# Taking a pair's two rounds of products apart, with the spread of the row sums between and behind them

## What is computed

```
h1     = concat(k, g, outer(k, g))            # 32 + 32 + 1024
act    = sigmoid(h1 @ W1 + b1)                # 36 hidden units
weight = act @ W2 + b2                        # one number for each goods row
out    = sum over the 200 rows of g * weight  # [2048, 32]
```

## Time and profile before

| | us |
|---|---|
| median of 3 runs | 266.45 (266.11 to 266.81) |
| profiled execution, its own time | 265.84 |
| span of the profiled execution | 264.0 |
| PE busy | 252.4 |
| ACT busy | 236.6 |
| POOL busy | 196.8 |
| DVE busy | 193.7 |

### The profile page before, as it was taken

How to read it: one execution, slowest core, us unless ns; L and a number is a source line. 1 busy time by engine, 2 the same in 40 slices (tenths; PEclk the granted TensorE clock), 3 DMA queues, 4 the chain that set the end, 5 groups by cost and what they waited for, 6 DMA issues and landing times.

```text
span 264.0 us, 18277 instructions
## 1 busy us (share of the span) xinstructions
PE 252.4 (96%) x7492; PEld 148.1 (56%) x7492; DVE 193.7 (73%) x1108; ACT 236.6 (90%) x658; POOL 196.8 (75%) x349
## 2 busy tenths in 40 slices
PE   7998999999999999999999999999999999999960
PEld 2425656555656656666556566566665565665640
DVE  0890277677778777777777787787787777877886
ACT  2897999999999999999999999999999999999840
POOL 1300787778888888888888888888888888888872
PEclk9999999999999999999999999999999999999997
DMA  5881767767777788777677787787777787777200
GB/s 207 263 298 38 218 190 217 219 203 241 216 227 237 216 240 234 217 235 224 220 237 217 235 230 222 233 233 215 233 226 219 233 233 229 226 222 232 63 0 11
DMA packets 38196, 54.84 MB, mean 208 GB/s; under 512 B 4241, under 2 KB 37905, under 8 KB 38033
## 3 DMA queue, kind: packets, MB, share of 16 engines
q1 hardware_dynamic: 37872, 54.15, 68.1%
q10 hardware_dynamic: 288, 0.32, 0.4%
HBM read 54.19 MB, written 0.26 MB: 206 GB/s over the span
## 4 chain that ended last, share of the span: by engine, by line
PE 91%; ACT 2%; DMA 2%; DVE 2%; POOL 1%; issue 0%; POOLq 0%; DVEq 0%
PE z_ps L337 29%; PE w_ps L384 27%; PE x_ps L360 16%; PE s_ps L422 6%; PE x_ps L422 6%; PE z_ps L289 2%; ACT act L498 2%; DMA act<-w_outer 2%; PE s_ps L337 2%; DVE goods L538 2%; PE s_ps L289 1%; PE x_ps L289 1%; PE x_ps L302 1%; PE w_ps L289 0%; POOL top L255 0%
## 5 line engine op out<-in xcount | busy, mean ns | idle before, releaser
L498 ACT ACTIVATE act<-z_ps,bias 128x200 f32<-128x200 f32 x448 | 149.8, 440 | 10.7 <-PE z_ps L337 4.3
L538 DVE CUSTOM_DVE_ANT_0 goods<-s_ps,goods 128x200 f32<-128x200 f32 x248 | 80.5, 362 | 30.9 <-PE w_ps L422 30.9
L337 PE MATMUL z_ps<-goods,wm_ring 32*32 32x200 f32 x3360 | 78.1, 339 | 0.1
L255 POOL TENSOR_SCALAR top<-whole,consts 128x200 bf16<-128x200 f32 x64 | 50.1, 783 | 21.7 <-DVE whole L530 15.6
L337 PEld LDWEIGHTS z_ps<-goods,wm_ring 32*32 32x32 f32 x3360 | 44.7, 103 | 20.1 <-issue 11.3
L384 PE MATMUL w_ps<-act,consts 128*32 128x200 f32 x1008 | 55.7, 339 | 0.0
L538 DVE CUSTOM_DVE_ANT_0 goods<-x_ps,goods 128x200 f32<-128x200 f32 x124 | 40.4, 364 | 20.6 <-PE s_ps L422 20.6
L360 PE MATMUL x_ps<-goods,wx 128*32 128x200 f32 x1024 | 55.3, 333 | 0.0
L259 POOL TENSOR_SCALAR mid<-rest,consts 128x200 bf16<-128x200 f32 x64 | 50.1, 783 | 6.3
L538 DVE DVE_READ_ACCUMULATOR2_ANT out_stage<- 128x1 f32 x512 | 42.7, 83 | 0.0
L422 PE MATMUL s_ps<-stack,pick_sb 64*128 64x200 bf16 x248 | 42.3, 251 | 0.0
(11 more groups left out here) (53 smaller groups left out, 210.6 us busy)
## 6 DMA issues: line engine op xcount, KB each, us to landing
goods<-goods_t SPq DMA_DIRECT2D x256, 200.0 KB, 2.9
act<-cand_r SPq DMA_DIRECT2D x1, 1024.0 KB, 5.3
act<-cand_u SPq DMA_DIRECT2D x1, 256.0 KB, 2.7
out_t<-out_stage SPq DMA_DIRECT2D x4, 64.0 KB, 2.4
consts<-small ACTq DMA_DIRECT2D x1, 164.5 KB, 5.3
act<-w_outer ACTq DMA_DIRECT2D x1, 144.0 KB, 5.5
pick_sb<-pick SPq DMA_DIRECT2D x1, 128.0 KB, 2.6
```

The costliest lines, as they stand in the source:

```text
L255: nc.gpsimd.tensor_scalar(top[:, :], whole[:, q % 2, :], m1, None, ALU.mult).then_inc(part_step, 1)
L337: last = nc.tensor.matmul(z_bank(slot, r)[32 * c:32 * c + 32, N * s:N * s + N], weights(slot, 32 * r, 4 * s + c), goods[32 * r:32 * r + 32 ...
L498: last = nc.scalar.activation(act[:, p % A_SLOTS, r, N * s:N * s + N], z_bank(p, r)[:, N * s:N * s + N], ACT.Sigmoid, bias=bias[:, r, p, s ...
L538: last = nc.vector.tensor_tensor_reduce(goods[:, q % G_SLOTS, v, :], s_bank(q, f, s)[:, N * i:N * i + N], goods[:, q % G_SLOTS, v, :], 1.0 ...
```

## The change

- In `products` the rounds are separate calls. The order on PE is now: round 0, spread f = 0, round 1, spread f = 1, `row_sums`, `products_x`.
- The spread has other banks: `w_ps` and `s_ps[1]` for f = 0, `x_ps` and the fourth bank of the pair before for f = 1. So round 0 waits, beside `goods_loaded` and `z_read`, for `pooled[1][1]` of the pair before; `products_x` waits for `pooled[1][0]` and `row_sums` for `pooled[0][0]` of the same pair's spread.
- DVE takes both halves of `pool_units` first and `keep` after them.
- `wm` is laid out in twos of hidden units: one copy of a bank now writes every second element, and a copy to the ring reads and writes neighbours in twos. Pairs 0 to 3 read the ring too; DVE fills their four places (`of_ring`), and raises `ring_filled`.
- GpSimd's operations are as before.

The core of the diff:

```diff
-        wm = sb("wm", [P, UNITS // RUN, HM, RUN])
+        wm = sb("wm", [P, UNITS // RUN, HM // 2, RUN, 2])
...
+        def s_banks(q, f):
+            if q + LAG >= PAIRS:
+                z0, z1, z2, z3 = (z_ps[:, r, :] for r in range(4))
+                return (((z0, z1), (z2, z3)), ((s_ps[1], x_ps), (z0, z1)), ((z2, z3), (s_ps[1], x_ps)))[q + LAG - PAIRS][f]
+            return ((w_ps, s_ps[1]), (x_ps, z_bank(q + LAG - 1, 3)))[f]
...
-            def products(p, slot, loaded):
+            def products(p, slot, s, loaded=None):
                 pe.wait_ge(pick_loaded, 16)
-                pe.wait_ge(goods_loaded[slot % G_SLOTS], loaded)
-                if slot >= 1:
-                    pe.wait_ge(z_read, p)
-                for s in range(2):
-                    ...
+                if s == 0:
+                    pe.wait_ge(goods_loaded[slot % G_SLOTS], loaded)
+                    if slot < FILL:
+                        pe.wait_ge(ring_filled, slot + 1)
+                    if slot >= 1:
+                        pe.wait_ge(z_read, p)
+                    if slot >= LAG + 1:
+                        pe.wait_ge(pooled[1][1], p)
+                ...
...
-                    products_x(p, slot)
-                    spread(p, slot, 1)
+                    products_x(pe.snap(pair, min_val=FILL - 1, max_val=PAIRS - 1), slot)
...
-                    products(p, slot + 1, pe.snap(loaded, min_val=64, max_val=64 * (TURNS + 1)))
+                    products(p, slot + 1, 0, pe.snap(loaded, min_val=64, max_val=64 * (TURNS + 1)))
                     spread(p, slot + 1, 0)
+                    products(p, slot + 1, 1)
+                    spread(p, slot + 1, 1)
                     row_sums(p, slot + 1)
...
+            for p in range(FILL):
+                if p == 2:
+                    keep_biasx()
+                nc.vector.tensor_copy(*of_ring(p)).then_inc(ring_filled, 1)
...
                 if q >= 0:
                     pool_units(q, 0)
-                if 1 <= p <= PAIRS:
+                    pool_units(q, 1, PAIRS - 1 if p == PAIRS else None)
+                if 1 <= p < PAIRS:
                     keep(p - 1)
-                if q >= 0:
-                    pool_units(q, 1)
```

More of the change, by code:

```diff
@@ L134, in wm_units, with of_ring @@
         def wm_units(h):
-            return wm[:, :, h, :]
+            return wm[:, :, h // 2, :, h % 2]
         def wb_runs(i, x):
             return wb_bank(i, x).rearrange("j (a b) -> j a b", b=RUN)
+        def of_ring(p):
+            first = p * PAIR_U % RUN
+            units = wm[:, p * PAIR_U // RUN, :, first:first + PAIR_U, :]
+            return (wm_ring[:, p % RING, :, :].rearrange("j u (g e) -> j u g e", e=2),
+                    units.rearrange("j g u e -> j u g e"))
         consts_loaded = sem("consts_loaded")
@@ L153, in build @@
         bias_kept = sem("bias_kept")
+        ring_filled = sem("ring_filled")
         z_done = sem("z_done")
@@ L314, in _ @@
             pe.wait_ge(pick_loaded, 16)
[L318 to L323, removed]
-            def products(p, slot, loaded):
-                pe.wait_ge(pick_loaded, 16)
-                pe.wait_ge(goods_loaded[slot % G_SLOTS], loaded)
-                if slot >= 1:
-                    pe.wait_ge(z_read, p)
-                for s in range(2):
[L335 to L342, removed]
+            def products(p, slot, s, loaded=None):
+                pe.wait_ge(pick_loaded, 16)
+                if s == 0:
[6 more added lines that the diff above has]
+                        pe.wait_ge(pooled[1][1], p)
+                for r in range(4):
+                    for c in range(4):
+                        last = nc.tensor.matmul(z_bank(slot, r)[32 * c:32 * c + 32, N * s:N * s + N],
+                                                wm_ring[32 * r:32 * r + 32, slot % RING, 4 * s + c, :],
+                                                goods[32 * r:32 * r + 32, slot % G_SLOTS, 4 * s + c, :],
+                                                start=True, stop=True)
+                    if s == 1:
+                        last.then_inc(z_done, 1)
             def products_x(p, slot):
@@ L351, in products_x @@
                 if slot >= LAG:
-                    pe.wait_ge(pooled[0][0], p)
-                elif slot >= 1:
-                    pe.wait_ge(actx_done, p)
+                    pe.wait_ge(pooled[1][0], p)
                 for s in range(2):
@@ L383, in row_sums @@
                             left, right = w2x[:, t, :], actx[:, a, :]
-                        last = nc.tensor.matmul(sums_bank(slot - 1)[32 * t:32 * t + 32, 0:N], left, right,
+                        last = nc.tensor.matmul(w_ps[32 * t:32 * t + 32, 0:N], left, right,
                                                 start=step == 0, stop=step == 2)
@@ L421, in spread @@
                         rows = slice(64 * s, 64 * s + 64)
-                        last = nc.tensor.matmul(s_bank(q, f, s)[:, N * i:N * i + N], pick_sb[rows, 2 * f + i, :],
+                        last = nc.tensor.matmul(s_banks(q, f)[s][:, N * i:N * i + N], pick_sb[rows, 2 * f + i, :],
                                                 stack[rows, q % 2, :], start=True, stop=True)
@@ L426, in _ @@
             for p in range(FILL):
-                products(p, p, 64)
+                products(p, p, 0, 64)
                 if p >= LAG:
                     spread(p, p, 0)
+                products(p, p, 1)
+                if p >= LAG:
+                    spread(p, p, 1)
                 if p >= 1:
@@ L479, in to_ring @@
             def to_ring(p):
-                first = p * PAIR_U % RUN
-                if p >= FILL + RING:
+                if p >= RING:
                     sc.wait_ge(z_done, 4 * (p - RING + 1))
-                units = wm[:, p * PAIR_U // RUN, :, first:first + PAIR_U]
-                nc.scalar.activation(wm_ring[:, p % RING, :, :], units.rearrange("j h u -> j u h"), ACT.Identity)
+                nc.scalar.activation(*of_ring(p), ACT.Identity)
             sc.wait_ge(wb_kept[0], kept(T_MAIN, 2))
@@ L529, in keep, with pool_units @@
                     dve.wait_ge(part_step, 3 * (p - 2) + 2)
-                nc.vector.tensor_scalar(whole[:, p % 2, :], sums_bank(p)[:, 0:N], b2, None, ALU.add).then_inc(w_kept, 1)
-            def pool_units(q, f):
+                nc.vector.tensor_scalar(whole[:, p % 2, :], w_ps[:, 0:N], b2, None, ALU.add).then_inc(w_kept, KEPT_FROM + 1 if p == 0 else 1)
+            def pool_units(q, f, amid=None):
                 dve.wait_ge(s_done, 2 * q + f + 1)
                 for s in range(2):
+                    if s == 1 and amid is not None:
+                        keep(amid)
                     for i in range(2):
```

54 lines of the change are left out of this document (23 added, 31 removed).

## The result

The changed kernel takes 275.69 us (median of 4 runs, 275.24 to 276.31) against 266.28 for the kernel before on the same chip: ratio 1.0352, 95% interval 1.0323 to 1.0381. It is slower by 9.4 us. The forecast was slower by 3.9, 270.4 within 265.2 to 273.5: the sign holds, the size does not, and the time lies outside the range. The profiled execution took 276.31, its span 274.5. TensorE's granted clock was 0.992 of full speed over it (0.993 before), so the clock has no part in the difference.

A forecast was written before the change was run, and what follows sets the result against it. PE was taken to bound the kernel before, ACT's cycle the changed one at 3.69 us a pair. Loop +3.8, pairs 1 to 3 -0.2, end +0.3 gave +3.9 us: 266.45 to 270.4, range 265.2 to 273.5.

The forecast's parts named there:

- PE's list: PE's stages of one pair in the steady loop, predicted to sum to 3.49 us, 0.14 less a pair.
- The reading of round 0 as queued and round 1 as fed late: In products, round 1 behind its own spread would be queued too: 0.55 us each round, 1.10 instead of 1.24.
- the fifth change of form: One more tile form change a pair on PE, taken as already paid for in the 3.49 us.
- The cycle through ScalarE: From one z_read to the next: 3.63 us without the fourth wait's price, 3.69 with it; forecast chance 0.54.
- I take the middle, 0.06: Price a pair of round 0's fourth wait, pooled[1][1] behind z_read, between nothing and 0.11 us.
- from round 1's load to the first sigmoid: Term of the cycle through ACT: 0.20 to the second halves, 0.02 to the fourth, 0.42 to the sigmoid; 0.64 us.
- bank copies over 800 ns: Sign that the prediction is wrong; copies into wm were expected to stay near 740 ns.
- wm in twos: Bank copies writing at steps of 8 bytes, taken to cost nothing; bounds nothing or 6.5 us.
- hidden in the wait for ACT: products_x, 0.12 us late behind six DVE units, leaves PE's list at 3.61 to 3.64, under 3.69.
- Without that cover it would cost: If the wait for ACT did not hide it, products_x's lateness would cost 0.12 us a pair.
- Pairs 1 to 3: At the start, bound by ACT's cycle, they lose the scattered reading of wm: -0.2 us together.
- the end: keep of pair 62 comes 0.5 us later, 0.17 comes back on POOL: +0.3 us.

The follow-up runs named there:

- e8: e7 with VectorE taking the two units in x_ps fourth and fifth, so products_x gets its bank one unit sooner: 266.48 us, ratio 1.0002.
- e10: e8 with bank 2 last in round 0, only its matmuls waiting for z_read, the others for ScalarE's fourth sigmoid: 270.44 us, ratio 1.0161.
- e1: Changed kernel with the wait for z_read written last in round 0 instead of second to last: 270.79 us, ratio 1.0167.
- e3: Changed kernel with the second sigmoid of bank 1, ahead of z_read, cut to 20 columns in pairs from 4 on: 268.13 us, one run.
- e6: Changed kernel with z_done waited for ahead of w_done at the first sigmoid of a pair: 272.05 us, ratio 1.0219.
- e4: Changed kernel with the second sigmoid of bank 3, behind z_read, cut to 20 columns: 276.86 us, one run.
- e5: Changed kernel with VectorE's first pooled unit of each pair cut to 20 columns: 275.92 us, one run.
- e9: e8 with the old layout of wm: 266.66 us, ratio 1.0005.
- e11: e9 with bank 2 last in round 0, as in e10: 270.92 us, ratio 1.0175.
- e12: Kernel before with a fourth, long fulfilled wait behind z_read ahead of the products: 266.86 us, one run, against 266.24 for the kernel before.
- e7: Changed kernel with the wait edits of e1 and e6 together: 268.56 us, ratio 1.0088.
- e2: Changed kernel with the two rounds of products joined again and both spread halves behind them: 308.46 us, one run.

## Why the prediction was right in sign and wrong in size

**PE's list.** Predicted 0.55, 0.28, 0.55, 0.28 for the four new stages; measured 0.59, 0.28, 0.56, 0.28. The reading of round 0 as queued and round 1 as fed late held, and the fifth change of form costs no more than is in these lengths, as e8's shorter pair shows too. The Trainium skill (TensorE: Matmul & The Clock Gate) states a queue of 64 entries; the trace after agrees, with both rounds of 64 records at 0.55 to 0.59. The four stages together went from 1.80 to 1.70 (medians). The list as a whole was put too short all the same: the step from products_x to round 0 was taken as the old 0.96 and needs 1.01 where it waits for nobody (e10), so that some 0.08 a pair were to be had, not 0.14.

**The cycle through ScalarE** was named as what takes it back, and that was right: e1, e3 and e6 move the time with its terms and nearly by the amounts, e4 and e5 outside it don't. Its terms, in the order of the prediction: release 0.11 + 0.06, round 0 0.58, spread 0.28, round 1 to the first sigmoid 0.64, sigmoids 2.02, in all 3.69. Measured: 0.22 (127.00 to 127.22), 0.59 (127.22 to 127.81), 0.28, 0.67 (128.09 to 128.76), 2.02: 3.78.

**The step that failed** is "I take the middle, 0.06" for the fourth wait: it costs its upper bound, 0.10 to 0.11. That is 0.05 x 60 = 3 us. The other 0.04 a pair are two small terms that were read too low: from round 1's load to the first sigmoid (0.67 for 0.64) and round 0 (0.59 for 0.58). In the first, the second halves start 0.20 behind the load as read (124.31 to 124.51), but the sigmoid comes 0.47 behind them (124.98) and not 0.44; why is open. In a cycle that closes at the old period to the hundredth, each hundredth is 0.6 us, and the range should have been worked out from all five terms and not from the fourth wait alone. 60 x 0.15 = 9 us is then nearly the whole result. The sum had a slip of its own, without weight: 60 x 0.06 is 3.6 us, not 3.8. Of the signs of being wrong, one came true, bank copies over 800 ns, and the period lay above the 3.66 to 3.73 that was to show the forecast right.

**The start.** wm in twos was put at nothing. DVE's bank copies and the ring copy held to that, ACT's did not. Groups by form after, beside the earlier trace rows:

```profile
L479 ACT ACTIVATE wm<-s_ps,consts 128x512 f32<-128x512 f32 x4 | 3.4, 850 | 0.0
...
L523 DVE TENSOR_SCALAR wm<-s_ps,consts 128x512 f32<-128x512 f32 x4 | 3.0, 746 | 0.0
...
L535 DVE COPY wm_ring<-wm 128x256 f32<-128x256 f32 x4 | 1.0, 287 | 0.2 <-ACT wm L479 0.2
```

850 against 731 ns on ACT, 746 against 750 on DVE; the first products came at 20.60 instead of 20.13. That is +0.5 us. It is the layout and not DVE's filling of the ring: in the traces with the old layout (before, e9, e11, e12) the first products come at 20.13 to 20.28, though DVE fills the ring in e9 and e11, and in those with the new one at 20.36 to 20.79. The Trainium skill (SBUF — State Buffer, the note on cachelines) asks for two hits to each 16-byte line; DVE's copies and the ring copy agree, and ACT's writes, which have the two hits and cost 0.12 more, don't. There the measurement decides.

**The other waits.** products_x was put 0.12 late and "hidden in the wait for ACT". It was late by about 0.1 in two pairs of three and by 0.19 in the third, whose extra wait for `wx_laid` I had overlooked (the cause is read from the program, not tested); that it is hidden was right (e5). "Without that cover it would cost" was right too, and dearer: in e7 the cover is gone and the period is 3.67 on average, not 3.61 to 3.64. Pairs 1 to 3 gave back 0.1 (0.2 predicted), and the end, put at +0.3, cost nothing that the traces show: from the row sums of pair 63 to the end both take 12.9.

**What stays open.** e8 has the shorter period than before (3.61 to 3.63, -0.8 us over 60 pairs) and a start 0.3 later, so -0.5 was to be expected; its ratio of 1.0002 (0.9971 to 1.0033) doesn't exclude that. In its profile the loop's first turn is dear: from the row sums of pair 4 to those of pair 10 it takes 25.6 us, where the kernel before takes 23.0 and e8's own period would give 21.7. The longest rounds of products there take 1.65 us, and the profile names nothing that they wait for but issue. But that execution, 268.58, was the slowest of e8's twelve, 2.1 above their median, so part of these 25.6 may belong to it alone. e9's profile, also its slowest (267.57), has 25.4; all others but the joined rounds of e2 (26.4, at 4.3 a pair) have 22.1 to 24.6. Why a first turn is slow, and whether it is more so in this order, wasn't tried.

## What to carry to other kernels

When a stage is split to make one engine's list shorter, add up the cycle that goes out through another engine and back, wait for wait, and not the list alone: here the list lost about 0.1 us, and the cycle came to 0.15 over the old period. On a cycle that binds, the order in which waits are written is worth as much as array work: the wait that is fulfilled last goes where no further sequencer step follows it. With 0.4 us between the semaphore and the instruction the same step was all but free (e12). And before a wait is moved in among the matmuls, ask whether TensorE could have started them any sooner (e10).

## What the runs showed of the hardware that I had not expected

- A weight load with four waits, z_read written as the third of them, starts 0.22 us behind the end of the releasing sigmoid; with z_read written last 0.11 (changed kernel and e1). Between matmuls of one round, a further pair of waits made the round 0.13 longer (e10).
- On ScalarE, the first sigmoid with the older wait written first cost 0.06 of each pair (e6: 3.78 to 3.72).
- ScalarE took 0.12 us more for writing 512 float32 at steps of 8 bytes than side by side (731 to 850 ns), VectorE nothing (750 to 746).
- The 32 records of one round of float32 32x32 matmuls take 0.55 us from load to the next form's load when they stand behind a change of form, and added 0.69 behind another round.
